# Attention layers on one core: GpSimd's split of the next body's x waits for VectorE's last low half of the exponentials

## The reference, cut to what matters

```
x = layernorm(x + mean_h(softmax(x Wq_h (x Wk_h)^T / sqrt(512)) x Wv_h) fc^T + b)
x = layernorm(x + causal_cross_attention(x, ctx) Wout^T)
x = layernorm(x + experts(x) + silu(x sg^T) * (x su^T) sd^T)
```

## Time and profile before

| | us |
|---|---|
| median of 3 runs (2083.06 to 2096.1) | 2085.97 |
| the profiled execution | 2088.78 |
| its span, from the first to the last instruction | 2087.0 |

### The profile page before, as it was taken

How to read it: one execution, slowest core, us unless ns; L and a number is a source line. 1 busy time by engine, 2 the same in 40 slices (tenths; PEclk the granted TensorE clock), 3 DMA queues, 4 the chain that set the end, 5 groups by cost and what they waited for, 6 DMA issues and landing times.

```text
span 2087.0 us, 43336 instructions
## 1 busy us (share of the span) xinstructions
PE 1988.5 (95%) x16976; PEld 1226.5 (59%) x16976; DVE 1703.1 (82%) x3877; ACT 1026.5 (49%) x1569; POOL 735.4 (35%) x710
## 2 busy tenths in 40 slices
PE   8999999999999999999999997899999999999997
PEld 3666666665676576575566564445555555555553
DVE  5567988988988988988988888848888888888767
ACT  5425434444443443453453454536566566665544
POOL 1003223223223322323322322344455555564543
PEclk9999999999999999999999998999999999999999
DMA  6700011010011011011011014278999999999948
GB/s 232 68 24 26 30 54 32 24 54 32 27 52 45 21 45 54 12 45 54 12 44 55 12 43 143 102 209 271 283 303 289 303 292 300 299 282 299 280 79 323
DMA packets 134439, 268.84 MB, mean 129 GB/s; under 512 B 32699, under 2 KB 42939, under 8 KB 134236
## 3 DMA queue, kind: packets, MB, share of 16 engines
q1 hardware_dynamic: 110108, 226.06, 33.1%
q0 software_dynamic: 24128, 40.01, 9.9%
HBM read 208.67 MB, written 57.42 MB: 127 GB/s over the span
## 4 chain that ended last, share of the span: by engine, by line
PE 50%; DVE 32%; issue 6%; ACT 5%; DMA 4%; POOL 2%; POOLq 0%; DVEq 0%; ACTq 0%
PE moe_bank L1708 21%; PE ring L916 16%; DVE quad L1296 6%; DVE inv_denominator L1312 4%; PE moe_bank L1777 4%; DVE scratch L1260 3%; DMA expert_sums<-tion_then_expert_weights,scatter_index 3%; PE fold L485 2%; DVE scratch L1306 2%; DVE stats L1221 2%; DVE maxima L1296 1%; PE quad L1031 1%; ACT scratch L1178 1%; PE moe_bank L1743 1%; POOL scratch L886 1%
## 5 line engine op out<-in xcount | busy, mean ns | idle before, releaser
L178 POOL DMA_INDIRECT slot_table<-table_records,slot_of_choice x204 | 202.1, 991 | 583.4 <-PE ring L916 399.7
L1158 ACT ACTIVATE scratch<-ring 128x512 f16<-128x512 f32 x224 | 131.6, 594 | 323.1 <-PE ring L916 322.8
L916 PE MATMUL ring<-xT_split,tion_then_expert_weights 128*128 128x256 f16 x2304 | 267.3, 273 | 0.0
L916 PE MATMUL ring<-tion_then_expert_weights,xT_split 128*128 128x512 f16 x1152 | 264.6, 379 | 0.0
L916 PEld LDWEIGHTS ring<-xT_split,tion_then_expert_weights 128*128 128x128 f16 x2304 | 220.6, 98 | 38.8 <-issue 10.2
L886 POOL TENSOR_SCALAR_AFFINE_SELECT scratch<-scratch 128x1024 f32<-128x1024 f32 x64 | 95.6, 1493 | 312.4 <-ACT scratch L1178 308.5
L1657 POOL DMA_INDIRECT expert_sums<-tion_then_expert_weights,scatter_index x64 | 131.8, 2060 | 197.7 <-DMA expert_sums<-tion_then_expert_weights,scatter_index 61.7
L916 PEld LDWEIGHTS ring<-tion_then_expert_weights,xT_split 128*128 128x128 f16 x1152 | 110.3, 98 | 125.7 <-DVE scratch L1260 2.9
L1296 DVE CUSTOM_DVE_ANT_0 quad<-quad,causal_penalty 128x128 f32<-128x128 f32 (+1 forms) x512 | 165.4, 399 | 1.8 <-PE quad L1014 1.7
L1260 DVE SCALAR_TENSOR_TENSOR scratch<-ring,scratch 128x512 f16<-128x512 f32 x192 | 128.2, 687 | 42.1 <-ACT scratch L1158 40.8
L916 PE MATMUL ring<-scratch,xT_split 128*128 128x256 f16 x1152 | 136.0, 272 | 10.7 <-DVE maxima_T L1303 6.4
(11 more groups left out here) (251 smaller groups left out, 4066.4 us busy)
## 6 DMA issues: line engine op xcount, KB each, us to landing
gate_up_landing<-in_w_gate SPq DMA_DIRECT2D x43, 704.0 KB, 5.7
gate_up_landing<-in_w_up SPq DMA_DIRECT2D x43, 704.0 KB, 5.9
scratch<-in_w_down SPq DMA_DIRECT2D x43, 512.0 KB, 4.8
scratch<-in_w_gate SPq DMA_DIRECT2D x21, 704.0 KB, 5.8
scratch<-in_w_up SPq DMA_DIRECT2D x21, 704.0 KB, 5.7
tion_then_expert_weights<-in_w_down SPq DMA_DIRECT2D x21, 512.0 KB, 4.5
scratch<-in_w_down SPq DMA_DIRECT2D x43, 192.0 KB, 6.1
xT_in<-in_xT SPq DMA_DIRECT2D x16, 512.0 KB, 4.9
```

The lines of the kernel that those rows point to most:

```text
L178: pool.indirect_dma_start(self.dram, bass.IndirectOffsetOnAxis(ap=self.slot[:, tb, c:c + 1], axis=0), self.record[:, tb, c, :], None, boun ...
L916: last = pe.matmul(out_, left(a, c), right(b, c), start=(n == 0 and not onto), stop=(n == 3 * chunks - 1))
L1158: act.activation(half(0), src, ACT.Copy, scale=scale).then_inc(high, 1)
```

## The change

`XS` gets one more wait, in bodies 2 to 15: the number of `pready` signals of all cross-attention steps before body i, so that the fourth low half of body i-1 (`P 3`, L1306) must be done. Body 1 has no cross-attention before it, and is left out.

```diff
                 if name == "XS" and not b.is_(0):
                     pool.wait_ge(xT_loaded, b.n(16, 0, 0, 16))
                     pool.wait_ge(full, b.last_job(*X_READERS[-1]))
+                    if not b.is_(1):
+                        pool.wait_ge(pready, b.n(0, 4, 0, 0))
                     own_wait(pool, taken)
                     pool.tensor_copy(xs[:, 0, :, :], xT_in[:, :, :]).then_inc(xfer, 1)
```

## The result

| | before | changed |
|---|---|---|
| median of 19 runs, us | 2091.2 (2082.3 to 2119.18) | 2072.17 (2053.23 to 2093.85) |
| ratio, 95% interval | | 0.9879 [0.9844, 0.9914] |
| span of the profiled execution, us | 2087.0 | 2064.9 |

The change makes the kernel faster by 1.2%, which is 25 us of the 2086 on which the prediction was made, with an interval from 18 to 33; 28 were forecast. The ratio and its interval leave out the runs counted as slow (over 1.5% above the fastest of their kernel, 3 of the 19 of the changed kernel), so they are not the ratio of the two medians, which lie only 19.0 us apart (0.9909). Both kernels spread over some 40 us in these runs, and the lowest times are 2082.3 - 2053.23 = 29.1 us apart.

The account below looks back on a forecast made before the run. TensorE was nearly full at 95%, but VectorE, slowed by GpSimd's splits, set the end of a body. Terms -29.1 + 1.0 = -28.1 us, from the median 2085.97, gave 2058, range 2052 to 2068.

Parts of the forecast that it names:

- What goes: End of a body: the pair and L1306 no longer lie beside GpSimd's splits; 2.05 us a body, 29.1 us in all.
- The extra 0.40 us of body 1: In body 1 the pair took 2.85 us, 0.40 more, so 2.45 us goes there instead of 2.05.
- TensorE keeps pace: Output projection starts 8.37 us after the pair instead of 10.43, with a 0.39 us gap left; the whole shift carries over.
- The new place: Splits just fit between OM 1 and OM 2; cost 0 to 0.52 us a body, taken as 0.07, 1 us in all.
- Who waits for GpSimd: Later readers of GpSimd's work: 7.5 us free before TensorE reads the new x, scatters and masks catch up; cost nothing.
- Carried to the whole time: Whole kernel: 28.1 us taken off the median of 2085.97 gives 2057.9, stated as 2058.
- A: Splits collide with OM 1 or OM 2 in the new place; 7 or 14 us given back, 2064 to 2072; chance 12%.
- B: Every VectorE instruction writing SBUF waits for GpSimd, so the splits stop the divisions; +30 us, 2116; chance 4%.
- C: TensorE takes up the gap or late scatters hold something; 2072 if half is lost, 2083 if nearly all; chance 8%.

Follow-up runs that it names:

- the floor: Kernel before, without the new wait, splits of bodies 2 to 15 cut to 1 column of each 256 of x and 4 of the context: body 74.65 us.
- one step earlier: Kernel before, with the split of x waiting for the last pair of self-attention weights' low halves instead of P 3: body 75.51 us, changed kernel 74.63.

## Why the prediction was right

*What goes, 2.05 us a body and 29.1 us in all.* Right. Body 15, which has no split of x, was a true picture of the other bodies without it: the pair and L1306 take 0.87 and 1.75 in both. The body lost 2.07 us, the stage 29.4 by the first traces, and 1154.5 - 1124.8 = 29.7 by the means of three each. The extra 0.40 us of body 1 were right too: from the start of its pair to the end of the low half it took 181.65 - 176.65 = 5.00 us and now 180.62 - 178.08 = 2.54, 2.46 less against 2.45. That the lowest whole times lie just 29.1 apart is chance; in the later sessions they are 27.4 and 28.5 apart.

*TensorE keeps pace.* Right. The output projection starts 559.79 - 551.42 = 8.37 us behind the pair, the very number of body 15, with the same gap of 0.39 us ahead of it.

*The new place, 0 to 0.52 us a body, taken as 0.07.* It measured 0, by the floor of 74.65 us. The split's last instruction ends 7.13 us behind the pair's start and `OM 2` starts 7.23 behind it, against 7.2 and 7.24 in the forecast. One detail was wrong: the copy was to show about 1.2 us, as it waits for `OM 1` inside its record. It shows 1.04, since it begins only 0.26 us after `L1308` ends, when `OM 1` is all but done (554.29). The sum doesn't depend on it.

*Who waits for GpSimd: nobody.* Right. The first scatter moved to 7.3 us behind the pair, 8 were forecast, and from the fourth on the scatters wait for TensorE as before; `MASK 0` still waits for ScalarE.

*Carried to the whole time.* The forecast of 2058 rested on a median of 2085.97 from three runs. Nineteen runs of the same kernel have 2091.2, and the changed kernel's 2072.17 lies 4 us above the range that was given, 2052 to 2068. In proportion the forecast, 2058 / 2086 = 0.9866, lies inside the measured interval. Of the 14.2 us between 2072.17 and 2058, 5.2 are the median of before, which three runs had put too low, and 9.0 are that the medians moved by 19.0 us and not by 28. What was mis-sized is the spread of the runs, put at 3 us on either side: the experts' stage alone varies by 23 us in three traces of one kernel, by the stalls shown above. The prediction had no term for that stage.

*The rivals.* A (the splits collide in their new place) is refuted for this change by the floor, but it is a real mechanism: one step earlier it costs 0.88 us a body, by just the way described, the copy going ahead of `OM 1`. B (divisions wait too) is refuted: L1312, now L1314, beside the long subtraction, keeps 1741 to 1759 ns in its 64 runs. C (the shift is lost further on) is refuted for the attention stage; for the experts' stage the traces show a variation that both kernels have.

## What to carry to other kernels

Look for instructions of VectorE and GpSimd whose records are longer in one place than in another, and for "issue" time in the chain between two parts of one group: here that was waiting which no releaser names. The cure here was not less work but another moment, and it was worth as much as leaving out the work (74.63 against 74.65 us a body): put GpSimd's SBUF work beside VectorE instructions that read PSUM, and let it become ready just behind, not during, the VectorE instruction that precedes that stretch. Where VectorE has one SBUF input, look at its records there too, as L193 waited and BN_STATS did not. A body of a loop that happens to lack the suspected work is an experiment that the trace has already run.

## What the runs showed of the hardware that was not expected

- A VectorE `tensor_scalar` of 128x2 with a single SBUF input waited for GpSimd's subtraction (0.59 us instead of 0.17), while BN_STATS of 128x512 with a single SBUF input, beside the same subtraction, kept its time (1.29 us for two).
- A GpSimd copy that became ready during a VectorE instruction took its turn ahead of VectorE's next one (2.31 us for the copy, 1.26 instead of 0.41 for the VectorE instruction), though that one stood ready in the queue.
- A waiting instruction's record ended 0.13 to 0.14 us before the other's end plus its own length, in four meetings (`MASK 1`, L1306, the copy and `OM 1` one step earlier).
- The time from the last P low half to the end varied from 767.3 to 790.1 us in three traces of one kernel on one core; 15.2 us of the longest were TensorE waiting, behind VectorE, for an indirect DMA that adds to `expert_sums`.
